# Second retention: the gate added to the normed output on GpSimd, one output product instead of two

## The reference

```
mu, var = mean(ret), var(ret) over a head's 16 channels
ret     = (ret - mu) * rsqrt(var + EPS)
ret     = ret.reshape(B, S, 128) * gn_w + gn_b
gated   = x @ W1
out     = gated * sigmoid(gated) + ret
return  out @ W2
```

## Time and profile before

| what | value |
|---|---|
| runs shown | 1224.97, 1221.35, 1225.27 us (median 1224.97) |
| the profiled execution, its own time | 1221.15 us |
| its span, first to last instruction | 1219.3 us, 31631 instructions |
| PE busy | 1120.4 us (92%) |
| DVE busy | 902.7 us (74%) |
| ACT busy | 742.4 us (61%) |
| POOL busy | 732.1 us (60%) |
| mean granted clock of PE | 0.965 |

### The profile page before, as it was taken

One profiled execution on the slowest core, in us unless ns is written; L12 is line 12 of the kernel. 1 busy time (PEld: TensorE's weight loads), 2 busy tenths in 40 slices (PEclk: granted clock), 3 DMA queues, 4 the chain that ended last, 5 costly groups with the idle time before them and its releaser, 6 DMA issues.

```text
span 1219.3 us, 31631 instructions
## 1 busy us (share of the span) xinstructions
PE 1120.4 (92%) x10400; PEld 999.5 (82%) x10400; DVE 902.7 (74%) x2648; ACT 742.4 (61%) x2015; POOL 732.1 (60%) x901
## 2 busy tenths in 40 slices
PE   7999999997788999978999999877899999999991
PEld 5888888885778999956777777666899999999991
DVE  4788998898756777756888888864676666667873
ACT  2345444653555777745667878744566666667884
POOL 0247777776467777473466676566644444445765
PEclk9999999999898999999999999976999999999996
DMA  8222111201224433343232211111322112114553
GB/s 243 69 62 73 47 41 52 73 28 54 58 80 122 133 108 106 110 163 101 72 110 63 69 54 46 45 34 49 98 56 57 56 56 58 56 54 125 152 181 123
DMA packets 75423, 101.77 MB, mean 83 GB/s; under 512 B 15138, under 2 KB 51490, under 8 KB 74850
## 3 DMA queue, kind: packets, MB, share of 16 engines
q1 hardware_dynamic: 49538, 59.89, 17.2%
q0 software_dynamic: 17280, 35.69, 8.8%
q10 hardware_dynamic: 8448, 4.20, 1.2%
HBM read 59.87 MB, written 43.04 MB: 84 GB/s over the span
## 4 chain that ended last, share of the span: by engine, by line
PE 66%; DVE 17%; ACT 5%; issue 4%; POOL 3%; SPq 1%; DMA 1%; ACTq 1%; DVEq 0%; POOLq 0%
PE banks L2351 16%; PE banks L2370 10%; PE banks L1444 6%; PE banks L1462 4%; DVE a_sT L1116 3%; PE banks L2279 2%; PE banks L1383 2%; PE banks L1353 2%; PE banks L2288 2%; ACT a_r_x L260 1%; PE banks L2317 1%; PE banks L2296 1%; PE banks L1380 1%; POOL expert_out L897 1%; DVE a_qm L1218 1%
## 5 line engine op out<-in xcount | busy, mean ns | idle before, releaser
L1866 POOL DMA_INDIRECT expert_out<-e_ysb,b_e_idx x142 | 161.8, 1139 | 152.1 <-ACT e_ysb L1971 124.7
L2351 PE MATMUL banks<-b_e_x_hi,e_w_hi 128*128 128x256 f32 x568 | 167.1, 294 | 3.9 <-ACT e_sgl L1961 2.3
L897 POOL DMA_INDIRECT expert_out<-a_e_ysb,a_e_idx x142 | 141.3, 995 | 44.4 <-issue 34.6
L2351 PE MATMUL banks<-b_e_x_hi,e_w_lo 128*128 128x256 f32 x568 | 160.2, 282 | 0.0
L477 POOL DMA_INDIRECT scattered<-a_r_x,a_r_idx x128 | 128.1, 1001 | 33.9 <-issue 33.9
L2370 PE MATMUL banks<-w_dn,e_h 128*128 x1136 | 138.3, 275 | 2.3 <-DVE e_h L2163 2.3
L2370 PEld LDWEIGHTS banks<-w_dn,e_h 128*128 128x128 f32 x1136 | 132.5, 192 | 3.0 <-issue 2.9
L2163 DVE TENSOR_TENSOR e_h<-banks,e_sgl 128x512 f32<-128x512 f32 x142 | 97.1, 689 | 50.5 <-PE banks L2351 47.9
L1961 ACT ACTIVATE e_sgl<-banks 128x512 f32<-128x512 f32 x142 | 85.2, 600 | 75.3 <-DVE e_h L2163 41.8
L477 POOL DMA_INDIRECT scattered<-b_r_x,b_r_idx x112 | 111.2, 992 | 30.8 <-issue 30.8
L2151 DVE TENSOR_TENSOR e_w_lo<-w_gu,e_w_hi 128x1024 fp32r<-128x1024 f32 x71 | 87.0, 1226 | 54.0 <-ACT e_w_hi L1950 53.9
(11 more groups left out here) (385 smaller groups left out, 3284.3 us busy)
## 6 DMA issues: line engine op xcount, KB each, us to landing
a_e_xg<-scattered SPq DMA_DIRECT2D x71, 130.0 KB
b_e_xg<-scattered SPq DMA_DIRECT2D x71, 130.0 KB, 2.1
b_cy<-expert_out SPq DMA_DIRECT2D x32, 256.0 KB, 3.3
f_y<-expert_out SPq DMA_DIRECT2D x32, 256.0 KB, 3.9
a_xT<-in_x_T SPq DMA_DIRECT2D x16, 256.0 KB, 2.9
out<-f_x ACTq DMA_DIRECT2D x16, 256.0 KB, 3.5
expert_out<-a_e_ysb,a_e_idx POOLq DMA_INDIRECT x142, 2.3
expert_out<-e_ysb,b_e_idx POOLq DMA_INDIRECT x142
```

Of the source, the lines that this page charges most:

```text
L897: nc.gpsimd.indirect_dma_start(out=expert_out, out_offset=bass.IndirectOffsetOnAxis(ap=idx[n % HELD][:, i:i + 1], axis=0), in_=ysb[n % HEL ...
L1866: nc.gpsimd.indirect_dma_start(out=expert_out, out_offset=bass.IndirectOffsetOnAxis(ap=idx[n % 4][:, i:i + 1], axis=0), in_=ysb[n % 4][:, ...
L2351: mm = nc.tensor.matmul(bank_of(c, j)[:, i * ROWS:(i + 1) * ROWS], w_[c % RING][:, g, f:f + P], x_[c % RING][:], start=(m == 0), stop=(m = ...
```

## The change

`gated_sum` is new on POOL: once `oT` and the gate `sgT` of the same sequence are there, it adds the gate to `oT` in place. `project_out` then needs one product per chunk instead of two, and waits for that sum alone. For that the norm's weight gn_w has to be in `oT` already: it becomes the per-channel scale of ACT's copy from `O` to `oc`. The matrix `w_2g` goes. In a full step `gated_sum` stands on POOL behind the two norms' powers; in step 19 it stands behind the eight scatters. It has a semaphore of its own, and the first layer has one store slot, and one semaphore, less: 16 instead of 17.

```diff
-        HELD = 17
+        HELD = 16
...
                             nc.scalar.copy(w_2[:], W_BANK[:, 0:P]).then_inc(w2_there, 1)
-                            nc.scalar.activation(w_2g[:], W_BANK[:, 0:P], ACT.Copy, scale=g_w[:, 0:1]).then_inc(w2_there, 1)
...
-                            pe.wait_ge(w2_there, 2)
+                            pe.wait_ge(w2_there, 1)
...
+                    def gated_sum(c1):
+                        pool.wait_ge(oT_there, c1.n + 1)
+                        pool.wait_ge(sg_there, c1.n + 1)
+                        nc.gpsimd.tensor_tensor(oT[:], oT[:], sgT[c1.odd][:], ALU.add).then_inc(osum_there, 1)
...
                         if c2:
                             norm.power(pool, c2)
+                        if c1:
+                            gated_sum(c1)
...
                             for q in range(4):
                                 if e:
                                     router.scatter_pair(pool, e, q)
+                            if c1:
+                                gated_sum(c1)
                             fill(2)
...
-                            nc.scalar.copy(oc[:], O[:, :]).then_inc(oc_there, 1)
+                            nc.scalar.activation(oc[:], O[:, :], ACT.Copy, scale=g_w[:, 0:1]).then_inc(oc_there, 1)
...
                     def project_out(c2):
-                        pe.wait_ge(oT_there, c2.n + 1)
-                        pe.wait_ge(sg_there, c2.n + 1)
+                        pe.wait_ge(osum_there, c2.n + 1)
...
                         for i in range(CH):
-                            nc.tensor.matmul(T0[:, i * D:(i + 1) * D], sgT[c2.odd][:, i * P:(i + 1) * P], w_2[:],
-                                             start=False, stop=False, skip_group_check=True)
-                            mm = nc.tensor.matmul(T0[:, i * D:(i + 1) * D], oT[:, i * P:(i + 1) * P], w_2g[:],
+                            mm = nc.tensor.matmul(T0[:, i * D:(i + 1) * D], oT[:, i * P:(i + 1) * P], w_2[:],
                                                   start=False, stop=True, skip_group_check=True)
...
-            w_v, w_2, w_2g = (shared_sb(n, [P, P]) for n in ("wv", "w2", "w2g"))
+            w_v, w_2 = (shared_sb(n, [P, P]) for n in ("wv", "w2"))
```

More of the change, by code:

```diff
@@ L1744, in second_layer @@
                 var_mm, var_there, ex_mm, oT_there = sem("var_mm"), sem("var_there"), sem("ex_mm"), sem("oT_there")
+                osum_there = sem("osum_there")
                 yb_there = sem("yb_there")
@@ L2270, in _ @@
                     pe.wait_ge(first.wv_there, 1)
-                    pe.wait_ge(first.w2_there, 2)
+                    pe.wait_ge(first.w2_there, 1)
                     pe.wait_ge(first.set_there, 2)
```

## The result

The change makes the kernel slower: 1238.08 us (median of 4 runs, 1234.46 to 1241.86) against 1224.36 for the kernel before on the same chip (4 runs, 1221.35 to 1225.27), a ratio of 1.0123 with a 95% interval of 1.0103 to 1.0143. That is 13.7 us. The forecast was 1232.7, the upper end of its range 1238.0. The profiled execution took 1241.86, the slowest of its four; its span is 1240.0 against 1219.3 before.

A forecast was written before the change was run, and what follows sets the result against it. PE and DVE were taken to bound the kernel as a ring with 0.32 us of DVE slack; -11 x 0.32 + 13 x 1.0 - 1.7 + 1.7 = +9.5 us on 1223.2 gave 1232.7, range 1218 to 1238 (forecast's own 1228 to 1237).

The forecast's parts named there:

- The ring: Second retention, steps 6 to 16: PE and DVE wait on each other in turn; DVE's 0.32 us slack caps the gain per step.
- the hold-up: Full steps: DVE's `pick` or `picked` delayed by POOL's add on SBUF, taken as 1.0 us per step.
- The add's 1.25 us: POOL's 128x512 `gated_sum`: assumed 1.25 us, between two passes over the data and three, with ends of 0.6 and 1.44.
- The exclusion that also holds DVE: Steps 6 to 18: two-operand SBUF instructions on POOL and DVE exclude each other both ways, delaying DVE 1.0 us in 13 steps.
- A short hold-up: Rival for the full steps: DVE delayed only 0.25 to 0.6 us, about +1 us in all, 1224; chance 0.20.
- none: Rival for the full steps: POOL's add does not delay DVE, only gains stay, 1219.2 or 1217 us; chance 0.25.
- The power with the undelayed `a_kT`: Trace evidence against DVE being delayed: two-operand `a_kT` runs undelayed at 0.68 us inside POOL's 16-column power of 3.41 us.
- The parts at zero: Scaled `oc` copy, one store slot fewer in the first layer, no `w2g` setting up: each forecast to change the time by 0.
- The drain: Steps 19 and 20: projection of 14 gains 1.7 us, that of 15 loses 1.7 waiting for POOL's add behind eight scatters.
- The sum of +9.5: Whole kernel: -11 x 0.32 + 13 x 1.0 - 1.7 + 1.7 = +9.5 us.
- with about 1.6 us more idle per step PE could lose its clock: Rival for the full steps: one step's PE work at half clock costs some 15 us, 1240 and up; shared chance 0.05.
- a spoilt cover: Rival on POOL: the add is held past its 2.34 us idle time and pushes the scatters, 1240 and up; shared chance 0.05.

## Why the prediction was right and where it fell short

- **The ring with 0.32 us of slack** on DVE: right. With the hold-up gone the steps come down by 0.37, not by 0.9, while PE has 0.83 us less to do.
- **The add's 1.25 us**: 1.25 to 1.28 in all 16.
- **The exclusion that also holds DVE, 1.0 us in 13 steps**: right. `pick` is 1.03 longer in steps 6 to 16, `dif` 0.8 and 1.0 in steps 17 and 18. The step grows by 0.69; the forecast had 1.0 - 0.32 = 0.68. A short hold-up and none, rivals with 0.45 between them, are out: the delay goes with the length of the reading add (0.72 and 1.26) and vanishes with a fill. The power with the undelayed `a_kT`, which spoke for no hold-up, is 16 columns; that it only reads for a small part of its time was argued, and no run was made for it. The lines above show a second such case: `dif`, which reads two SBUF operands, stands inside the power of 4 columns (652.65 to 653.66) at its plain 0.17.
- **The parts at zero** (scaled copy, 16 slots, setting up `w2g`): right as far as tried; the first two were measured together at 1.0003, the third was not tried alone.
- **The drain**: `b_r` of 15 came 19.1 us after that of 14; 18.9 was forecast. That it was avoidable, by a place between the scatters, the forecast didn't see.
- **The sum of +9.5**: the mechanism measured +9.8 in the profile and 10.6 us with PE kept busy (1234.57 - 1223.98). The agreement isn't one of errors that cancel: stretch by stretch, the forecast's terms come to -0.3 for step 6, +6.8, +1.0 for step 17, +1.0 for step 18, -0.7 for the projection of 14 (1.0 of hold-up less 1.7) and +1.7, against -0.4, +7.0, +0.9, about 1.05, -0.7 and +1.95. In the line of the projection of 14 the hold-up and the four products were not measured apart.
- **What failed is the step that gave the clock no term in the sum.** The prediction named it among the rivals ("with about 1.6 us more idle per step PE could lose its clock"), gave it, together with a spoilt cover, 0.05, and priced a whole step at half clock, 15 us. The runs showed both together: the idle time grew by 1.5 us, and in three or four steps of ten the clock fell for a part of the step and cost 1.62 each. The products that kept PE busy took 4 to 6 us off the median. Of the 5.4 us between the forecast's 1232.7 and 1238.1, 4.2 (13.7 - 9.5) is what the sum lacked, most of it the clock; the other 1.2 is the start, 1223.2 in the forecast and 1224.36 in the runs of the kernel before. It wasn't a case beside the forecast's: the hold-up itself makes the idle time on PE, and the trace before already showed the clock at half in the drain, where PE is busy for 11.08 of 17.00 us. Whether so much idle time would cost the clock could not be read there: with 1.26 us idle in a step (half the add, one profile) no step lost it.

## What to carry to other kernels

A free stretch in one engine's queue is not a free place: look at what the other engine does at that moment, and put an elementwise instruction on GpSimd beside DVE work that reads PSUM or one SBUF tensor; the same add was worth +1.2% in one gap and -0.4% when each was put into another. A delay in a ring that PE turns can be paid twice, as the delay and as clock, as it was here. So a forecast with more idle time on PE needs a term for the clock, even if only as a spread. In the drain here, the place of the add in a queue of slow scatters counted for more (3.6 us) than its length (1.26).

## What was not expected of the hardware

- DVE shows a held instruction as a longer one, not as a wait: `pick` "took" 1.26 us, with no idle time ahead of it, and the view of waits on DVE shows nothing. The sign is two instructions of different engines that end together.
- A fill of 512 columns on POOL took 0.54 us and the add 1.26, 0.72 for half: so the second 256 columns of the add took 0.54 us, or 2.1 ns a column with two operands read. The Trainium skill (GPSIMD Engine Reference, "Elementwise — side-by-side cycle accounting") has 4497 ns for an add of 2048 columns, from which 1.1 us is an estimate for 512; the measured 1.26 decides.
- Which steps run in part at half clock differs between executions of one program: steps 8, 12 and 14 in one, 8, 10, 11 and 13 in another.
